# A merged middle stage: where three weight splits, a bias split, a root, an exponential and four transpositions stand in their engines' queues

## The reference

```python
x = x + L1_ffn(layernorm(x))         # gate softmax, top 2 of 8 experts of rank 8, dense base
x = x + L2_xattn(layernorm(x), ctx, ctx)
x = x + L2_ffn(layernorm(x))         # top 2 of 4 experts of rank 16, no base
x = x + L3_xattn(layernorm(x), ctx)
...
def L2_xattn(q, k, v):               # 64 groups of 8 channels, linear attention
    qh = softmax(q, over the 8 channels of a group)
    kh = softmax(k, over the 512 channels of a token)
    kvs = einsum('bnhd,bnhe->bhde', kh, vh)
    return einsum('bnhd,bhde->bnhe', qh, kvs)
def L3_xattn(text, features):        # both normalised by root mean squares, with biases
    features_n = rmsnorm(features) * fn_w
    Q, K = rmsnorm(text @ Wq.T + bq) * qn_w, rmsnorm(features_n @ Wk.T + bk) * kn_w
    return softmax(Q K' / sqrt(512)) features_n
```

## Time and profile before

| | |
|---|---|
| median of 3 runs | 1514.89 us (1513.87 to 1515.61) |
| profiled execution, its own time | 1514.85 us |
| its span, first to last instruction | 1513.1 us |
| granted clock of TensorE, mean over the span | 0.992 |
| TensorE, VectorE, ScalarE, GpSimd busy | 1472.1, 1032.4, 926.9, 402.4 us |
| HBM read and written | 58.72 and 2.10 MB |

### The profile page before, as it was taken

How to read it: one execution, slowest core, us unless ns; L and a number is a source line. 1 busy time by engine, 2 the same in 40 slices (tenths; PEclk the granted TensorE clock), 3 DMA queues, 4 the chain that set the end, 5 groups by cost and what they waited for, 6 DMA issues and landing times.

```text
span 1513.1 us, 27936 instructions
## 1 busy us (share of the span) xinstructions
PE 1472.1 (97%) x9532; PEld 1316.5 (87%) x9532; DVE 1032.4 (68%) x2449; ACT 926.9 (61%) x3133; POOL 402.4 (27%) x461
## 2 busy tenths in 40 slices
PE   8999999999999999998999999999999999989997
PEld 7999999999999998887888888888888888877885
DVE  7556555655565557886777777777777788767776
ACT  4456455545564555547777777777777774466652
POOL 5112011301130102233232323232323242644431
PEclk9999999999999999999999999999999999989999
DMA  5000100010000100101111110101010101011101
GB/s 219 33 29 29 43 29 29 29 43 29 29 29 29 43 29 27 57 35 43 36 43 42 37 50 29 50 29 50 29 50 29 39 8 67 29 46 37 48 15 60
DMA packets 16115, 62.60 MB, mean 41 GB/s; under 512 B 2228, under 2 KB 3764, under 8 KB 10984
## 3 DMA queue, kind: packets, MB, share of 16 engines
q1 hardware_dynamic: 15976, 60.82, 11.5%
HBM read 58.72 MB, written 2.10 MB: 40 GB/s over the span
## 4 chain that ended last, share of the span: by engine, by line
PE 54%; issue 26%; DVE 9%; ACT 6%; POOL 4%; DMA 0%; SPq 0%; POOLq 0%; ACTq 0%; DVEq 0%
PE psY L958 12%; PE psQ L874 9%; PE psKV L898 7%; PE psSO L843 2%; PE psSO L945 2%; POOL wo L541 2%; PE psTP L859 2%; PE psTP L908 2%; PE psQ L859 1%; PE psQ L799 1%; PE psSO L844 1%; PE psTP L928 1%; PE psKV L814 1%; ACT prob L1487 1%; PE psQ L1245 1%
## 5 line engine op out<-in xcount | busy, mean ns | idle before, releaser
L958 PE MATMUL psY<-wo,oT 128*128 128x512 f32 x1536 | 378.2, 394 | 0.7 <-DVE oT L1943 0.2
L958 PEld LDWEIGHTS psY<-wo,oT 128*128 128x128 f32 x1536 | 278.8, 188 | 56.2 <-POOL wo L541 2.2
L541 POOL TENSOR_TENSOR wo<-stage_o,wo 128x512 fp32r<-128x512 f32 x68 | 87.2, 1313 | 310.3 <-ACT wo L1400 279.6
L1400 ACT ACTIVATE pT<-psTP 64x256 fp32r<-64x256 f32 (+1 forms) x192 | 86.5, 451 | 124.2 <-PE psTP L928 123.4
L1490 ACT ACTIVATE prob<-wide,neg_mx 128x128 f32<-128x128 f32 x256 | 99.7, 391 | 81.5 <-DVE neg_mx L2075 81.5
L1487 ACT ACTIVATE prob<-s_sb,neg_mx 128x64 f32<-128x64 f32 x256 | 85.9, 337 | 94.2 <-DVE neg_mx L2075 94.2
L1943 DVE TENSOR_TENSOR pT<-psTP,pT 64x256 fp32r<-64x256 f32 (+1 forms) x192 | 97.6, 508 | 67.3 <-ACT pT L1400 65.5
L665 POOL TENSOR_TENSOR rms<-ms_eps,minus_half 128x5 f32<-128x5 f32 (+1 forms) x64 | 74.2, 1159 | 230.6 <-DVE ms_eps L2088 229.8
L541 POOL TENSOR_TENSOR wq<-stage_q,wq 128x512 fp32r<-128x512 f32 x42 | 53.9, 1301 | 209.3 <-ACT wq L1400 156.6
L898 PEld LDWEIGHTS psKV<-wkv,arena 128*128 128x128 f32 x768 | 100.3, 190 | 6.8 <-DVE kT L2123 1.8
L874 PE MATMUL psQ<-wq,hT 128*128 128x512 f32 x384 | 103.8, 407 | 0.0
(11 more groups left out here) (329 smaller groups left out, 3489.9 us busy)
## 6 DMA issues: line engine op xcount, KB each, us to landing
stage_o<-in_wo SPq DMA_DIRECT2D x16, 1024.0 KB, 4.8
stage_q<-in_wq SPq DMA_DIRECT2D x15, 1024.0 KB, 5.1
stage_kv<-in_wkv SPq DMA_DIRECT2D x12, 512.0 KB, 3.6
stage_q<-in_ctx SPq DMA_DIRECT2D x16, 256.0 KB, 3.0
stage_o<-in_ctxT SPq DMA_DIRECT2D x2, 1024.0 KB, 4.8
stage_q<-in_base SPq DMA_DIRECT2D x2, 1024.0 KB, 4.9
stage_kv<-in_ctx SPq DMA_DIRECT2D x8, 256.0 KB, 3.0
out<-x_res SPq DMA_DIRECT2D x8, 256.0 KB, 2.2
```

The source lines that it names most:

```text
L541: g.tensor_tensor(dst[LO], stage, dst[HI].bitcast(f32), ALU.subtract).then_inc(ld[done or what + "_lo"], 1)
L958: m = mm(psY[:], oT[:, ol, h, :], wo[:, wl, h, :], start=h == 0 and i == 0, stop=h == HQ - 1 and i == 2)
L1400: copy = lambda o, i: nc.scalar.activation(o, i, ACT.Copy)
```

## The change

Seven edits, all to the order or the engine of work; no matmul is added or taken away.

1. The low parts of `FF[2]`'s gate and second-layer weights go from GpSimd (between its steps 2 and 3) to VectorE (the end of its step 3).
2. VectorE scales the key sums (`kv_normalise`) ahead of `eT_lo` in steps 1 to 4; from step 5 on it stands where it was.
3. The bias rows' low parts go from the end of VectorE's middle step 6 to the end of its `ffn_step` 5.
4. The context root's mean goes from VectorE's step 7 to its `ffn_step` 0, and the power from GpSimd's step 7 to ahead of its loop over norm 4.
5. ScalarE's copy of key weights slice 0 (`wk_hi(0)`) goes from `after1(10)` to `after1(7)`, and its wait for the expert products is taken out. The exponential of context tile 5 goes from the end of ScalarE's step 3 to step 4, behind `kvs_hi`.
6. ScalarE's `gate_exp` goes ahead of the query's exponential: behind `deviations(5)`, in step 7 ahead of it; in step 8 it stays where it was.
7. TensorE's `norm6_transpose` goes from the end of the step to a place between `gate_product` and `experts`.

```diff
# GpSimd
-            if t == 7:
-                pool.wait_ge(N3["ms_f"], 1)
-                g.tensor_tensor(rf, ms_rf, minus_half[:], ALU.pow).then_inc(N3["pw_f"], 1)
...
+        pool.wait_ge(N3["ms_f"], 1)
+        g.tensor_tensor(rf, ms_rf, minus_half[:], ALU.pow).then_inc(N3["pw_f"], 1)
         for n in range(NT):
             ln_rstd(4, n)
...
             if n >= 5:
                 middle_step(n - 4)
-            if n == 6:
-                low_wkv(28, 136)
-                low("wkv", (b2_rows(HI), b2_rows(LO)), stage_kv[:, :, 2 * P:4 * P], 31)
# TensorE, middle_step
                 gate_product(f, e)
+            if 0 <= e - 3 < NT:
+                norm6_transpose(e - 3)
             if 0 <= e - 1 < NT:
                 experts(f, e - 1)
...
                 i.then_inc(s["y_tr"], 1)
-            if 0 <= e - 3 < NT:
-                norm6_transpose(e - 3)
# ScalarE, after1
-            if 4 <= t < 7:
-                wk_hi(t - 3)
+            if 4 <= t < 8:
+                wk_hi((t - 3) % KT)
             if 4 <= t < 6:
                 ctx_exp(t - 4)
-            if t == NT + 2:
-                act.wait_ge(FS["experts"], 2 * NT)
-                wk_hi(0)
# ScalarE, middle_step
             if 1 <= t <= 4:
                 kvs_hi(t - 1)
+            if t == 4:
+                ctx_exp(t + 1)
             if 0 <= e - 2 < NT:
                 deviations(6, e - 2)
+            if t == 7:
+                gate_exp(f, e)
             if 0 <= t - 3 < NT:
                 deviations(5, t - 3)
+            if 0 <= e < NT and t not in (7, 8):
+                gate_exp(f, e)
...
-            if 0 <= e < NT:
+            if t == 8:
                 gate_exp(f, e)
...
-            if t + 2 < NT:
+            if t + 2 < NT and t != 3:
                 ctx_exp(t + 2)
# VectorE, ffn_step
+            if f.index == 1 and t == 0:
+                dve.wait_ge(N3["f_sq"], NT)
+                V.tensor_scalar(ms_rf, sq_f[:], 1.0 / D, RMS_EPS3, ALU.mult, ALU.add).then_inc(N3["ms_f"], 1)
+            if f.index == 1 and t == 5:
+                dve.wait_ge(ld["vec_hi"], 1)
+                for r in bias_row.values():
+                    lo = slice(r + 32, r + 33)
+                    i = sub_hi(pT[lo, 0], wide[lo], pT[lo, 1])
+                i.then_inc(ld["vec_lo"], 1)
# VectorE, middle_step
+            def kv_normalise():
+                ... (the six lines taken out below)
+            if 0 < t < 5:
+                kv_normalise()
             if t < 5:
                 eT_lo(t)
...
-            if 0 <= t - 1 < NT:
-                dve.wait_ge(s["kv"], t)
-                link(V.reciprocal(small[:, 12:13], sums[:, (t - 1) % 4:(t - 1) % 4 + 1]))
-                need(dve, s["kvs_lo"], t - 1)
-                own = 0 if t < NT else P
-                V.scalar_tensor_tensor(kvs, psK2[:, own:own + P], small[:, 12:13], block8[:], ALU.mult,
-                                       ALU.mult).then_inc(s["kvs"], 1)
+            if 5 <= t <= NT:
+                kv_normalise()
...
-            if t == 7:
-                (the two lines of the context root's mean)
-            if t == 6:
-                (the five lines of the bias rows)
+            if t == 3:
+                for k in range(2):
+                    dve.wait_ge(ld["wkv_hi"], 29 + k)
+                    sub_hi(wkv[:, LO, k, 0:136], stage_kv[:, k, 0:136], wkv[:, HI, k, 0:136]).then_inc(ld["wkv_lo"], 1)
+                dve.wait_ge(ld["wkv_hi"], 31)
+                sub_hi(b2_rows(LO), stage_kv[:, :, 2 * P:4 * P], b2_rows(HI)).then_inc(ld["wkv_lo"], 1)
```

More of the change, by code:

```diff
@@ L2391, in middle_step @@
             s, f, e, n = M, FF[2], t - 5, t - 9
+            def kv_normalise():
+                dve.wait_ge(s["kv"], t)
+                link(V.reciprocal(small[:, 12:13], sums[:, (t - 1) % 4:(t - 1) % 4 + 1]))
+                need(dve, s["kvs_lo"], t - 1)
+                own = 0 if t < NT else P
+                V.scalar_tensor_tensor(kvs, psK2[:, own:own + P], small[:, 12:13], block8[:], ALU.mult,
+                                       ALU.mult).then_inc(s["kvs"], 1)
+            if 0 < t < 5:
+                kv_normalise()
             if t < 5:
@@ L2421, in middle_step @@
                 ln_lo(5, t - 4)
-            if t == 7:
-                dve.wait_ge(N3["f_sq"], NT)
-                V.tensor_scalar(ms_rf, sq_f[:], 1.0 / D, RMS_EPS3, ALU.mult, ALU.add).then_inc(N3["ms_f"], 1)
             if t == 8:
@@ L2435, in middle_step @@
                 kT_lo(n - 1)
-            if t == 6:
-                dve.wait_ge(ld["vec_hi"], 1)
-                for r in bias_row.values():
-                    lo = slice(r + 32, r + 33)
-                    i = sub_hi(pT[lo, 0], wide[lo], pT[lo, 1])
-                i.then_inc(ld["vec_lo"], 1)
+            if t == 3:
[4 more added lines that the diff above has]
+                sub_hi(b2_rows(LO), stage_kv[:, :, 2 * P:4 * P], b2_rows(HI)).then_inc(ld["wkv_lo"], 1)
         def cross_attention(next_ln):
```

## The result

The changed kernel takes 1503.98 us (median of 6 runs, 1501.82 to 1504.85) against 1514.51 us (6 runs): a ratio of 0.9928, 95% interval 0.9917 to 0.9938. The forecast was 1502.0, with 1498 to 1509 as its range. The profiled execution has a span of 1502.4 us, 10.7 less than before.

A forecast was written before the change was run, and what follows sets the result against it. TensorE, busy 97% of 1513.1 us, was taken as the bound, so gains lie only in its waits and lower clock. Terms -3.3 - 1.1 - 7.4 - 1.3 + 0.1 = -13.0 took 1514.85 to 1501.85, so 1502 us; range 1498 to 1509.

The forecast's parts named there:

- Term A: Middle steps 2 to 4: earlier normalisation and context split close TensorE's two gaps, 1.68 + 1.64 us: -3.3 us (other end 2.4).
- With the low parts off GpSimd, the root is 1.2 us earlier: GpSimd's root for tile 0 of norm 5 no longer stands behind the low parts and comes 1.2 us sooner.
- Term B: Middle step 4, from its key product on: the clock's first fall does not come, -1.1 us if the clock holds.
- the 2.74 of 4.00 us that had held: TensorE's busy time at 704 us, where the clock stayed at 1.00; step 4 was expected above it, 3 in 4.
- Term C: Middle steps 5 to 8: earlier gate exponential and moved bias rows give four steps of 6.6 us, -7.4 us (other end -5.0).
- Term D: Middle steps 10 to 12: norm 6 transpositions fill TensorE's wait before the expert product, three times 0.45 us: -1.3 us.
- now they stand in that wait: Steps 10 to 12: norm 6's four transpositions, 0.45 us, fill the wait for the hidden low part.
- its lower bound: Steps 10 to 12: a gain of 0 from the moved transpositions, if the wait moves to them.
- Term E: Second expert layer: the context squares' mean adds one VectorE instruction before the gates, +0.1 us (0 to 0.2).
- the prediction's other sum: The three low parts on VectorE each sit out a GpSimd subtraction: 2.3 us, 1504.2 in place of 1501.9 if unhidden.
- a new fall of the clock: A clock fall stays or comes anew behind new waits in steps 4 and 8: +4, 1506 us; chance 0.22.
- my signs of being wrong: Middle clock under 1, ScalarE idle over 1 us before each step's gate exponential, or VectorE SBUF instructions of 1 us and more.

The follow-up runs named there:

- the run that had the wait without the fall: Changed kernel with low parts back on GpSimd, key sums late and ScalarE's exponential and copy in their old places: 1506.92 us.
- the second profile: The changed kernel run and profiled again without any edit: 1504.80 us, ratio 0.9915-0.9942 to the kernel before.
- the low-part kernel: Changed kernel with the low parts of gate and second-layer weights back on GpSimd: 1505.37 us, ratio 0.9927-0.9954 to the kernel before.

## Why the prediction held, and where not

*Term A* (-3.3): -3.27, S to step 4's key product from 18.10 to 14.83 us. The chain came as forecast: ScalarE's normalisation is 1.47 us sooner behind S (12.17 in place of 13.64; forecast 1.2 to 1.5), and the wait of 1.64 us behind it is gone. That the size is also the sum of TensorE's two gaps is chance: the first gap still stands, at 1.23 us in place of 1.68, because TensorE too comes to it a good 1.0 us sooner.

The parts of A were not right. The step that failed is "With the low parts off GpSimd, the root is 1.2 us earlier". Undone alone, the low parts move the root by 0.36 us and N5 by 0.14; they move the root by 1.11 us (11.29 to 12.40) only where the key sums are late too. The key sums, priced at 0.3 us for the root and at 1.1 behind the split (with the residual sum), move the root by 0.56, the key product by 1.07 and N5 by 1.87 us; ScalarE's order, priced at 1.2, moves them by nothing, 0.64 and 1.23. What I passed over was ScalarE: before, it stood idle for the late key sums (1.22 us in step 2) ahead of the query's exponential, and everything behind that, GpSimd's queue too, was late by as much. For the root I costed the edit by the instruction that it overtakes, not by the engine that waited for its result.

*Term B* (-1.1): -1.12, and 1.03 us in the run that had the wait without the fall. The clock held in step 4, as forecast; the ground given for it, more busy time than the 2.74 of 4.00 us that had held, does not carry (see the rival below).

*Term C* (-7.4): -7.71, steps of 6.5 us on average (6.6 forecast for each), singly 5.85 to 7.26. The gate's exponential and the bias rows are 7.3 us of it (33.33 of 33.77 us came back); the other 0.44, in step 5, belong to the first fall of the clock, B's.

*Term D* (-1.3) was mis-sized: 21.55 - 20.94 = 0.6. The step "now they stand in that wait" holds, but its lower bound came half true: in steps 11 and 12 the transpositions themselves wait 0.35 and 0.44 us for ScalarE's normalisation, because a step is shorter now.

*Term E* (+0.1): +0.06 from the end of the output projection to S, +0.15 in the second profile.

*The contention.* The three low parts took 1.10 us on VectorE, and GpSimd's two small instructions beside them 0.2 us more, where the prediction's other sum had 2.3. In the second expert layer the bias rows and GpSimd's scaling, 1.38 + 1.57 = 2.95 us one behind the other, ran side by side and were over in 2.16 us (1301.67 to 1303.83), each 0.44 us longer. The Trainium skill (SBUF — State Buffer, "Who interferes with whom") has such a pair lock each other out; the direction agrees, but by a lock for whole instructions they would need 2.95 us, and the measurement decides.

*The rival "a new fall of the clock"* came in part: the wait stands at the end of step 8, as I had named it, and the fall behind it in step 9, at 1.56 us in place of about 4. A clock under 1 in the middle was also one of my signs of being wrong. The fall hit the changed kernel in both its profiles, and with step 9's 0.38 us at full clock makes the 1.19 us lost there. Nine profiles have the same two waits (1.43 to 1.46 and 0.33 us) ahead of step 9; the clock fell in four and held in five. The busy time ahead, off which I read the clock (2.33 and 2.74 of 4.00 us), does not tell: in the 4 us ahead of step 9's fall, or of its place, TensorE was busy 2.21 to 2.24 us in all nine, and ahead of the projection's 3.25 to 3.29 us in all 14 profiles, of which seven fell. The windows at the projection (TensorE alone), of the changed kernel, which fell, and of the low-part kernel, which held:

```profile
1259.30:1263.30 4.00, 3.27 (x23) 1.00 0.99 376
```

```profile
1259.69:1263.69 4.00, 3.28 (x24) 1.00 0.96 373
```

What decides stays open. One thing the nine profiles do show: step 9 fell in four of the five whose projection had fallen, and in none of the four others. So few can't prove a link.

Without this fall the middle is 85.53 - 72.54 = 13.0 us shorter (the low-part kernel, 1313.14 to 1385.68), the forecast's sum. That is partly luck: D brought 0.7 us too little, C 0.3 too much, and step 9 at full clock is 0.38 shorter than before, which no term had. Of the 2 us between 1502.0 and the median, step 9's fall accounts for some 0.7 us (1.56 us in four of nine profiles): an estimate from these rows, not a measurement. The projection's fall can't be put down to the change, since its program is the same before; how often it falls there in the kernel before, a single profile doesn't show. The rest stays open.

## What to carry to other kernels

Cost a moved instruction by the engines that stand idle for its result, and follow their queues, before you cost what it overtakes; undo edits in pairs, since either of two may lift the same delay. Where an engine's queue has hardly a gap left (VectorE, six instructions in a row ahead of step 9), removing one wait for it brings the next. Where the clock may fall, compare stretches by the trace at equal clock, not medians.

## What was not expected of the hardware

One program, same waits, two clocks: the output projection at 1262 us, whose program no kernel here alters, took 2.98 to 3.03 us in 7 of 14 profiles and 4.57 to 4.59 in the others. With step 9's 7.44 or 9.0 us this makes 3.2 us, about the spread of the changed kernel's runs (1501.8 to 1505.2 us).

A fall can also cost next to nothing. A query product at 695 us took 2.98 or 2.99 us in 7 of the 14 profiles and 3.91 to 4.60 in the others, which had a fall there. The next product for keys and values begins 5.08 us behind its start in the former and 5.07 to 5.20 in the latter, because TensorE waits in between in any case. TensorE's timelines of the kernel before (fallen) and of the one with the key sums undone (not):

```profile
695.27 4.58 PE L874 MATMUL psQ<-hT 128*128 128x512 f32 x12
...
700.34 1.69 PE L898 MATMUL psKV<-wkv,arena 128*128 128x256 f32 x12 [0.27 <-DVE kT L2123]
```

```profile
695.27 2.98 PE L870 MATMUL psQ<-hT 128*128 128x512 f32 x12
699.50 0.44 PE L924 MATMUL psTP<-ident,prob 128*128 128x128 f32 x2 [1.24 <-DVE prob L2080]
700.35 1.69 PE L894 MATMUL psKV<-wkv,arena 128*128 128x256 f32 x12 [0.42 <-DVE kT L2122]
```

And step 4 from its key product on took 4.08 us at full clock with the key sums late and 4.07 us with the low parts late too and a clock of 0.80 from 1330 to 1335 us, because ScalarE's normalisation ended both (at 1334.67 and 1336.73 us, and N5 is at 1334.73 and 1336.78).
